# Masked attention stage: residual loads and result stores cut by place in a block of rows

## The reference

```python
x = x + xattn0(layernorm(x), ctx, causal_mask, padding_mask, Wq, bq, Wk, bk, Wv, bv, Wo, bo)
x = x + ternary_ffn(layernorm(x), w1, g1, w2, g2, w3, g3)
x = x + gamma * xattn1(layernorm(x), ctx, ctx)
x = x + swiglu_ffn(layernorm(x), w_gate_up, w_down)
```

## Time and profile before

| | |
|---|---|
| median of 3 runs | 1810.11 us (1808.15 to 1810.71) |
| the profiled execution | 1812.99 us |
| its span, first to last instruction | 1811.2 us |
| TensorE busy (matmul) | 1500.2 us, 83% |
| VectorE busy | 862.8 us, 48% |
| ScalarE busy | 713.0 us, 39% |
| GpSimd busy | 396.9 us, 22% |
| granted TensorE clock, mean | 0.912 |
| moved by DMA | 138.14 MB, 76 GB/s over the span |

### The profile page before, as it was taken

How to read it: one execution, slowest core, us unless ns; L and a number is a source line. 1 busy time by engine, 2 the same in 40 slices (tenths; PEclk the granted TensorE clock), 3 DMA queues, 4 the chain that set the end, 5 groups by cost and what they waited for, 6 DMA issues and landing times. The chain is left out here.

```text
span 1811.2 us, 23713 instructions
## 1 busy us (share of the span) xinstructions
PE 1500.2 (83%) x9156; PEld 687.6 (38%) x9234; DVE 862.8 (48%) x1318; ACT 713.0 (39%) x1292; POOL 396.9 (22%) x479
## 2 busy tenths in 40 slices
PE   3568888778787827888936999999599999999998
PEld 2334444345344313444421222222244444444443
DVE  6444735548457327777525666663263131221220
ACT  2143444444434516777722655655243021120120
POOL 4300101101000016676541322321353000000000
PEclk8678889889888859999975999999699999999999
DMA  5524253351542220100025444420442200100100
GB/s 137 96 89 90 97 144 86 107 118 59 143 88 77 76 105 7 37 34 18 18 66 162 141 118 123 136 83 25 163 119 80 70 1 1 69 0 0 47 1 24
DMA packets 89546, 138.14 MB, mean 76 GB/s; under 512 B 7496, under 2 KB 48008, under 8 KB 88912
## 3 DMA queue, kind: packets, MB, share of 16 engines
q1 hardware_dynamic: 76640, 111.54, 22.3%
q10 hardware_dynamic: 12800, 25.17, 4.4%
HBM read 105.85 MB, written 30.83 MB: 75 GB/s over the span
## 5 line engine op out<-in xcount | busy, mean ns | idle before, releaser
L488 DVE TENSOR_REDUCE a_negmax<-a_psX 128x4 f32<-128x1024 f32 x128 | 149.9, 1218 | 173.0 <-PE a_psX L682 172.4
L1425 DVE TENSOR_REDUCE c_negmax<-c_psA 128x1 f32<-128x512 f32 x256 | 165.9, 683 | 99.4 <-PE c_psA L1489 98.0
L373 ACT ACTIVATE a_probs<-a_psB 128x512 f32<-128x512 f32 x256 | 138.5, 593 | 148.6 <-PE a_psB L692 148.4
L1790 PE MATMUL d_psGU<-d_zt_lo,d_w_hi 128*128 128x512 bf16 x501 | 191.7, 383 | 4.8 <-POOL d_w_lo L1673 4.3
L1790 PE MATMUL d_psGU<-d_zt_hi,d_w_hi 128*128 128x512 bf16 x502 | 191.8, 382 | 3.0 <-ACT d_silu L1710 2.4
L1790 PE MATMUL d_psGU<-d_zt_hi,d_w_lo 128*128 128x512 bf16 x501 | 191.6, 382 | 0.6
L1372 ACT ACTIVATE c_probs<-c_psB 128x512 f32<-128x512 f32 x256 | 140.2, 595 | 109.1 <-PE c_psB L1502 109.1
L692 PE MATMUL a_psB<-a_qs,a_ks 115*128 115x256 bf16 x512 | 138.7, 402 | 46.0 <-ACT a_probs L373 40.4
L1710 ACT ACTIVATE d_silu<-d_psGU 128x512 f32<-128x512 f32 x64 | 38.2, 596 | 350.5 <-PE d_psGU L1790 350.4
L1754 DVE TENSOR_TENSOR d_h<-d_psGU,d_silu 128x512 f32<-128x512 f32 x64 | 44.3, 692 | 226.4 <-PE d_psGU L1790 226.2
L1489 PE MATMUL c_psA<-c_ks,c_qs 96*128 96x512 bf16 x256 | 105.1, 413 | 41.9 <-DMA c_qs<-q_scr 28.3
(11 more groups left out here) (214 smaller groups left out, 2609.2 us busy)
## 6 DMA issues: line engine op xcount, KB each, us to landing
a_tern_stage<-in_w ACTq DMA_DIRECT2D x32, 768.0 KB, 7.8
d_weight_stage<-in_w_last SPq DMA_DIRECT2D x24, 512.0 KB, 4.0
a_ks<-k_scr SPq DMA_DIRECT2D x24, 256.0 KB
a_qs<-q_scr SPq DMA_DIRECT2D x24, 256.0 KB
c_ks<-k_scr SPq DMA_DIRECT2D x48, 128.0 KB, 2.6
c_qs<-q_scr SPq DMA_DIRECT2D x48, 128.0 KB, 3.0
a_xz<-in_x SPq DMA_DIRECT2D x8, 512.0 KB, 18.4
a_ctx<-in_ctx_t SPq DMA_DIRECT2D x8, 512.0 KB, 12.8
```

What stands on the lines that cost most here:

```text
L373: act.activation(pr[:, e % 4, :, jj * P:(jj + 1) * P].rearrange("p r (a i) -> p a r i", a=2), B[:, u % 2, :].rearrange("p (a r i) -> p a r ...
L488: v.tensor_reduce(negm[:, u, :], X[:, 2 * (u % 2):2 * (u % 2) + 2, :].rearrange("p a (j k) -> p (a j) k", k=SEQ), AX.X, ALU.max, negate=Tr ...
L1425: v.tensor_reduce(negm[:, u:u + 1], A[:, u % 2, :], AX.X, ALU.max, negate=True)\
L1790: last = pe.matmul(GU[:, 2 * up + i % 2, :], wgu[wh][:, i, up, k, :], zt[zh][:, k, :], start=(k == 0 and j == 0), stop=(k == DC - 1 and j ...
```

## The change

The loads of `a_xr` and the stores from it are made one transfer for each place, four for a block in each direction, where there was one for each slot. A transfer has 64 rows of 2 KB as its two dimensions, where it had 2 x 64 rows. `place(tile, j)` gives the 64 partitions and the slot that hold place `j`. The counts that the semaphores `xr_loaded` and `stored` are compared with grow to fit. Places 0 and 1 wait for the first `x_updated` of the block, 2 and 3 for the second.

```diff
-        def rows(dram, b, t):
+        def rows(dram, b, j):
 
-            return dram[b * SEQ:(b + 1) * SEQ, :].rearrange("(i t j) d -> t j i d", t=ST, j=QJ // ST)[t]
+            return dram[b * SEQ:(b + 1) * SEQ, :].rearrange("(i j) d -> j i d", j=QJ)[j]
+
+        def place(tile, j):
+
+            half = j % (QJ // ST)
+            return tile[half * QI:(half + 1) * QI, j // (QJ // ST), :]
...
-                need(sp, s["stored"], b * ST * DMA)
-                for t in range(ST):
-                    sp.dma_start(xr[:, t, :], rows(x_in, b, t)).then_inc(s["xr_loaded"], DMA)
+                need(sp, s["stored"], b * QJ * DMA)
+                for j in range(QJ):
+                    sp.dma_start(place(xr, j), rows(x_in, b, j)).then_inc(s["xr_loaded"], DMA)
...
-                for t in range(ST):
-                    sp.wait_ge(s["x_updated"], ST * b + t + 1)
-                    sp.dma_start(rows(x_out, b, t), xr[:, t, :]).then_inc(s["stored"], DMA)
-            sp.wait_ge(s["stored"], BATCH * ST * DMA)
+                for j in range(QJ):
+                    sp.wait_ge(s["x_updated"], ST * b + j // (QJ // ST) + 1)
+                    sp.dma_start(rows(x_out, b, j), place(xr, j)).then_inc(s["stored"], DMA)
+            sp.wait_ge(s["stored"], BATCH * QJ * DMA)
...
-                pool.wait_ge(s["xr_loaded"], (b + 1) * ST * DMA)
+                pool.wait_ge(s["xr_loaded"], (b + 1) * QJ * DMA)
```

## The result

The changed kernel took 1801.17 us in the median (1797.67 to 1804.1, 8 runs), the kernel before 1809.77 us beside it (1807.46 to 1813.87, 8 runs). The ratio is 0.9953, with a 95% interval of 0.994 to 0.9966: 8.5 us faster, between 6.2 and 10.9. The forecast was 1802.2 us, 7.9 us faster.

What follows compares the result with a forecast made beforehand. Bound taken: SP's 10.0 us wait at L82, stage end, for stores on two engines while compute engines stand. 10.0 - 1.6 - 0.5 = 7.9 us saved, everything else 0: 1810.11 - 7.9 = 1802.2 us, range 1797.5 to 1805.5.

Steps and rivals of the forecast that it cites:

- 10.0 - 1.6 - 0.5 = 7.9 us: Stage end: SP's 10.0 us wait at L82 becomes 1.6, one added issue costs 0.5; bounds 7.1 to 8.3 saved.
- the longest landing of 10.4 us: Longest landing among transfers grouped under tensor `x`, taken to show the stage-end stores on two engines took long.
- all behind SP's start moves as one piece: Next stage's loads, statistics and first matmul (653.73, 656.43, 674.17) depend on SP's start alone and shift together.
- The extra issues: Inside the blocks, four stores and four loads issued instead of two each: cost 0, covered by SP's 251.0 us idle.
- the earlier loads: `a_xr` loads in the blocks, and `a_xz` and `a_ctx` some 8 us earlier: worth 0, nobody waits for them.
- The issue of `a_xz` behind the stores: SP's load issue after block 0's stores, blocked by a full queue: from 7.16 us to 0.4 to 0.5.
- A: Stage-end transfers run one behind another, four stores at 2.0 us each: 5.0 us saved, 1805.1 us; chance 0.08.
- B: Stores stay at two engines, so the 10.0 us remain and one issue is added: 1810.6 us; chance 0.03.
- C: In five blocks, earlier `a_xz` and `a_ctx` loads take bandwidth from `a_qs`: up to 14.2 us, 1816.4 us; chance 0.07.
- D: In six blocks, old stores hold back `a_qs`; the change saves 12.8 us more, 1789.4 us; chance 0.10.
- The wait at L234: SP's wait for a store before reloading `a_xr`, 73.9 us over seven times: nearly goes, a sign of being right.
- the times between the starts of the blocks: Spacing of block starts within the stage: unchanged, named as a sign of a right forecast.

Runs made afterwards that it cites:

- the second comparison: The full change repeated on the chip of the kernel by halves, against the kernel before: 1802.06 us against 1808.19 us, ratio 0.9965.

## Why the prediction was right

**The place.** The end of the stage was the only place where all engines stand until one of these transfers has landed. Block 7's stores alone give the gain (0.9956), everything but them gives none (0.9996). The 73.9 us of the same wait inside the blocks, seven times the size, were worth nothing, since they fell to 34.2 us and SP's next wait took the difference.

**The size.** Each part of 10.0 - 1.6 - 0.5 = 7.9 us has its measured counterpart. The wait at L82 fell to 1.8 us, not 1.6. The issue that is added is 0.5 to 0.6 us: four issues take 3.60 us where two took 3.03. Together 11.67 - 4.04 = 7.63 us, 0.3 us less than forecast and inside the bounds of 7.1 and 8.3. The measured 8.5 us (6.2 to 10.9) and, in the second comparison, 6.3 us (4.5 to 8.1) lie on both sides of it. One reading behind the term was wrong, though the sum does not use it: the longest landing of 10.4 us is not that of these stores. Up to 655 us that view has landings of 2.7 to 2.9 us only, the 10.4 us lie in the second stage, and the profile of before gives no landing for the stores from `a_xr` at all. That all behind SP's start moves as one piece holds only within the spread of 18.3 to 20.4 us from the first load to the first matmul; TensorE did start at the low clock in both kernels.

**The cause.** The forecast read two engines from a share of 0.13 and put the width down to the outer dimension. With the same four stores of 128 KB in a block, outer dimensions of 2, 4, 8 and 64 gave shares of 0.14, 0.25 to 0.27, 0.50 and 0.92. The Trainium skill (DMA: Bandwidth & Descriptors, "Why a DMA increments its semaphore by 16 and not by 1") states that a transfer uses the largest count of engines up to 16 that divides the outermost dimensions of both its patterns. By that rule it had to be 2, 4, 8 and 16, and the traces agree.

**What costs nothing.** The extra issues, the earlier loads, the moved work of GpSimd: 0 forecast, 0.9999 measured for the loads, 0.9996 for all but block 7's stores. The issue of `a_xz` behind the stores was forecast to fall from 7.16 us to 0.4 or 0.5; it takes 0.59. `a_xz` lands earlier, and nobody had waited for it.

**The rivals.** A (one transfer behind another, 5.0 us saved) is out, since 7.63 us were saved at the end of the stage. B (the width stays at two engines) is out by the share of 0.92. C (`a_qs` held up by the earlier loads) and D (`a_qs` held up by the old stores) are out by TensorE's waits for `a_qs`, 21.2 us before, 19.7 after, 18.9 with the stores held back.

**What was not foreseen.** Two of the signs named for a right forecast did not come as told. The wait at L234 was to go nearly, and 34.2 of its 73.9 us stayed; in the changed kernel the stores from `a_xr` still take 6.5 us in the median and up to 10.5 us to land. It cost nothing, because SP had idle time behind it all the same, and why these landings in the blocks stay long was not tried. And the times between the starts of the blocks were to be unchanged. They were not, by 2.7 us in all, and from one pair of profiles that could have passed for a gain of the change. It took a kernel that has the same transfers there to see that it was not.

## What to carry to other kernels

Look at who waits for the landing, not at how slow a transfer is: the same slow store costs nothing seven times, with SP idle behind it, and its full length once, where a stage ends with it. A DMA share that stands at a small multiple of 1/16 while bytes are waited for hints, as the 0.13, 0.25 and 0.50 did here, that the transfer runs on few engines. Then read the outermost dimension of its patterns and make it larger; here 8 brought all but 0.4 us of what 64 rows brought. And before a difference between two profiles is put down to a change, find the same stretch in a third kernel that lacks it there.

## What was not expected of the hardware

The issue of a load was held back by stores ahead of it that ran on two engines. The issue of the load of `a_xz`, in ns (min/median/max of eight, of which five follow stores); before, with the stores on 4 engines, and in the changed kernel:

```profile
L164 SPq DMA_DIRECT2D a_xz<-in_x x8: 378/6818/9003, 0.7 to 465.0; - x8
```

```profile
L173 SPq DMA_DIRECT2D a_xz<-in_x x8: 379/494/525, 0.7 to 467.8; - x8
```

```profile
L169 SPq DMA_DIRECT2D a_xz<-in_x x8: 379/587/594, 0.7 to 463.4; - x8
```

The median is 6818 ns, 494 ns and 587 ns. With stores on two engines ahead of it the load's issue took several microseconds, with stores on four it did not. It goes with the stores of the blocks and not with the loads of `a_xr`: the median was 7088 ns with only the loads by place and 7353 ns with only block 7 stored by place, both with the old stores in the blocks. Nor does it take loads of `a_qs` in the queue: where the stores waited until these had landed, the issue behind them still took 5.58 us (the row at 180.40 above). That the queues of the two engines were full, as the prediction has it, is the likely cause; no run tested it by itself.

The landing of ScalarE's `a_tern_stage`, which goes by another queue, had a median of 7.8 us and now has 4.8 us. It was 5.3 us with the old stores and only the loads by place, so the stores alone do not explain it; here too nobody waited.

The second surprise is the end at wide transfers: from 8 to 16 engines only 0.4 us are gained, and issuing the last transfer from a second queue gains nothing. The rows of the changed kernel split the 4.04 us between the last addition and the next load: 0.69 us for the addition itself, 1.11 us from its end to the end of the last issue, and 2.24 us until SP's next issue. In the last of these the DMA engines are busy up to 639.8 at the latest, and from there to 640.6 the share is 0.00. So at most 1.4 us of the 4.04 are time in which the stores' bytes move.
